# Four edits to a fused attention and mixture-of-experts kernel: wide rows for token numbers, an earlier residual load, merged masks, and one shared network moved from the tail into the last batch's body

## The reference, cut to what matters

```python
diff = a1 - lam * a2
out = einsum('bhts,bhsd->bhtd', diff, v)
out = (out - mean) * rsqrt(var + EPS)          # mean, var over all tokens of a head
h = layernorm(x + out @ Wo)                    # post-norm
router_logits = h @ router_w.T                 # top 1 of 8 experts
gate = sigmoid(topk_vals)
xs = h * gate
routed = w_down[e] @ silu_mul(xs @ w_gate_up[e])   # e: the token's expert
shared = silu_mul(h @ shared_gate_up) @ shared_down
out = layernorm(h + routed + shared)
```

## Time and profile before

| | us |
|---|---|
| median of three runs | 888.58 |
| the profiled execution, as timed | 890.63 |
| its span, first to last instruction | 888.9 |
| TensorE matmul busy | 761.6 |
| VectorE busy | 464.9 |
| ScalarE busy | 331.0 |
| GpSimd busy | 304.3 |

### The profile page before, as it was taken

The page is one execution under the profiler, slowest core; times in us unless marked ns, Lnnn a source line. Parts: engine busy times, 40 slices in busy tenths (PEclk is TensorE's granted clock), DMA queues, the critical chain, the costliest instruction groups (busy, mean ns, idle before and its releaser), DMA issues.

```text
span 888.9 us, 10662 instructions
## 1 busy us (share of the span) xinstructions
PE 761.6 (86%) x3590; PEld 381.9 (43%) x3590; DVE 464.9 (52%) x1036; ACT 331.0 (37%) x607; POOL 304.3 (34%) x262
## 2 busy tenths in 40 slices
PE   7187899997799989878998997899959867999994
PEld 3152234333244534523454353344226533666663
DVE  2765876751667765327767454774324421333332
ACT  2315443434564433255543334455613101222220
POOL 3038610123962121067510221211311204666653
PEclk9689999999799999987999899999969997999998
DMA  3753095002037220300731207000853102112100
GB/s 123 180 99 107 1 192 84 27 2 36 25 77 137 39 50 0 61 1 24 155 55 34 37 1 202 1 1 2 159 181 133 47 1 61 56 59 64 50 22 0
DMA packets 49333, 57.55 MB, mean 65 GB/s; under 512 B 11559, under 2 KB 43053, under 8 KB 47424
## 3 DMA queue, kind: packets, MB, share of 16 engines
q1 hardware_dynamic: 43024, 49.37, 25.0%
q0 software_dynamic: 3824, 6.32, 2.4%
q10 hardware_dynamic: 2432, 1.18, 0.5%
HBM read 42.67 MB, written 16.99 MB: 67 GB/s over the span
## 4 chain that ended last, share of the span: by engine, by line
PE 65%; DVE 10%; POOL 8%; DMA 7%; issue 6%; ACT 2%; SPq 0%; POOLq 0%; DVEq 0%; ACTq 0%
PE pv_ps L957 14%; PE wide_ps L1035 9%; PE s_ps L796 7%; PE wide_ps L943 7%; DVE mneg L1389 4%; PE wide_ps L783 4%; PE wide_ps L927 4%; DMA work<-x_in 3%; PE s_ps L797 3%; PE wide_ps L899 3%; PE pv_ps L1054 2%; PE misc L1054 2%; DMA slot_tokens<-tokens,slot 2%; PE misc L874 2%; PE s_ps L828 2%
## 5 line engine op out<-in xcount | busy, mean ns | idle before, releaser
L1389 DVE TENSOR_REDUCE mneg<-s_ps 128x1 f32<-128x384 f32 (+3 forms) x352 | 217.0, 638 | 105.2 <-PE s_ps L797 101.1
L1169 ACT ACTIVATE w_exp<-wide_ps 128x512 f32<-128x512 f32 x320 | 180.2, 599 | 118.9 <-PE wide_ps L943 117.6
L957 PE MATMUL pv_ps<-w_exp,work 128*64 128x512 f32 x640 | 182.3, 650 | 20.6 <-POOL w_exp L1302 18.6
L796 PE MATMUL s_ps<-w_exp 96*128 96x256 bf16 (+3 forms) x512 | 138.8, 313 | 33.5 <-DMA w_exp<-q_parts 18.3
L1302 POOL TENSOR_SCALAR_AFFINE_SELECT w_exp<-w_exp 128x1024 f32<-128x1024 f32 x64 | 70.7, 1105 | 280.7 <-ACT w_exp L1169 280.7
L943 PE MATMUL wide_ps<-w_exp 98*128 98x512 bf16 x320 | 124.0, 397 | 16.3 <-ACT w_exp L1169 15.0
L797 PE MATMUL s_ps<-mask,identb 128*128 128x128 bf16 x512 | 101.9, 227 | 0.0
L943 PEld LDWEIGHTS wide_ps<-w_exp 98*128 98x128 bf16 x320 | 31.8, 103 | 159.4 <-ACT w_exp L1169 101.3
L1035 PE MATMUL wide_ps<-w_exp,tables 128*128 x184 | 84.9, 605 | 0.0
L796 PEld LDWEIGHTS s_ps<-w_exp 96*128 96x128 bf16 x512 | 51.4, 101 | 70.9 <-DVE mneg L1389 38.8
L797 PEld LDWEIGHTS s_ps<-mask,identb 128*128 128x128 bf16 x512 | 52.3, 102 | 29.1 <-issue 5.9
(11 more groups left out here) (162 smaller groups left out, 1002.8 us busy)
## 6 DMA issues: line engine op xcount, KB each, us to landing
w_exp<-q_parts SPq DMA_DIRECT2D x96, 128.0 KB, 5.3
w_exp<-w_up_in SPq DMA_DIRECT2D x8, 1024.0 KB, 9.4
work<-x_in SPq DMA_DIRECT2D x8, 512.0 KB, 7.8
w_exp<-w_down_in SPq DMA_DIRECT2D x8, 512.0 KB, 11.5
q_parts<-w_exp SPq DMA_DIRECT2D x6, 512.0 KB, 7.0
w_exp<-k_parts SPq DMA_DIRECT2D x18, 128.0 KB, 4.0
gated_rows<-work SPq DMA_DIRECT2D x4, 512.0 KB, 3.1
x2s_rows<-x SPq DMA_DIRECT2D x4, 512.0 KB, 4.9
```

What stands on the lines that cost most here:

```text
L796: nc.tensor.matmul(o, q_stack[0:KROWS, qt, hs, :], keys[0:KROWS, gs, 0:qt + 1, :], start=True, stop=False)
L957: last = nc.tensor.matmul(pv_ps[s * 64:(s + 1) * 64, :], vo[:, kt, g, :], probs[:, n % NP, s, :], start=(kt == 0), stop=(kt == qt))
L1169: nc.scalar.activation(probs[:, n % NP, s], st_bank(v), ACT.Exp, scale=float(DH) ** -0.5).then_inc(st_done, 1)
L1389: nc.vector.tensor_reduce(out=mneg[:, qt, rows[0]:rows[-1] + 1], in_=s_ps[:, (v - 1) % 2, 0:len(rows) * w].rearrange("p (r k) -> p r k", r ...
```

## The change

Four edits.

1. **Rows of token numbers.** `slot_tokens` gets 64 equal numbers (256 bytes) for each place instead of one. VectorE spreads the numbers of a batch 64 times (`tokens_wide`, in the task `top`), and the scatter writes rows of 256 bytes. The table is filled beforehand with one number for "no token" by a DMA of 5.0 MB from SBUF on ScalarE's queue (`none_yet`), in place of a copy of 75.5 KB from DRAM. The read back takes the first number of each row.
2. **Residual load moved.** In the last body SyncE issues the residual load ahead of the loads of experts 2 and 3.
3. **Merged masks.** A bank of scores gets one mask matmul over all its rows instead of one for each.
4. **Shared network moved.** That of batch 2 goes through `SHARED` in the last body's steps 28 to 39, as in bodies 1 and 2; the `late_` tasks leave the tail. The semaphores are renamed from `late_` to `last_`.

```diff
-TAIL = [(_name, _arg, 1 if _name.startswith("late") else 0) for _name, _arg in (
-    ("norm", NUNIT - 1), ("sum", QT - 1), ("late_gate", 0), ("late_up", 0), ("mean", 0), ("late_gate", 1), ("late_up", 1), ("square", 0),
+TAIL = [(_name, _arg, 0) for _name, _arg in (
+    ("norm", NUNIT - 1), ("sum", QT - 1), ("mean", 0), ("square", 0),
...
     return [t for t in TASKS[n] if (t[2] == 0 and not (t[:2] in ONCE and post)) or (t[2] < 0 and ahead)
-            or (t[2] > 0 and post and (ahead or t[:2] not in SHARED))]
+            or (t[2] > 0 and post)]
...
-    slot_tokens = nc.dram_tensor("slot_tokens", ((E * NTOK + NROUTE) * P, 1), I32, kind="Internal").ap()
+    slot_tokens = nc.dram_tensor("slot_tokens", ((FILLS * E) * P, COPIES), I32, kind="Internal").ap()
...
-                sp.dma_start(slot_tokens, spare_d).then_inc(tokens_ready, 16)
...
                 if post:
                     store_gated(b - 1)
+                if not prep:
+                    load_residual(b)
...
-                load_residual(b)
                 if prep:
+                    load_residual(b)
                     max_rows(b + 1, 2, turned_maxima(b, 2, -1))
...
-            sp.wait_ge(late_added, QT)
+            sp.wait_ge(x2s_done, B - 1)
             store_x2s(B - 2)
...
-                sp.dma_start(rows_of[:, i:i + 1], slot_tokens[bass.ds(at * P, P), :]).then_inc(ids_loaded[g], 16)
+                sp.dma_start(rows_of[:, i:i + 1], slot_tokens[bass.ds(at * P, P), 0:1], allow_slow_non_contiguous=True).then_inc(ids_loaded[g], 16)
...
                 for n, hs in enumerate(rows):
-                    gs = hs // 4
-                    o = s_ps[:, (v - 1) % 2, n * w:(n + 1) * w]
-                    nc.tensor.matmul(o, q_stack[0:KROWS, qt, hs, :], keys[0:KROWS, gs, 0:qt + 1, :], start=True, stop=False)
-                    last = nc.tensor.matmul(o[:, w - P:w], identb[:], mask[:], start=False, stop=True)
+                    nc.tensor.matmul(o[:, n], q_stack[0:KROWS, qt, hs, :], keys[0:KROWS, hs // 4, 0:qt + 1, :], start=(n == 0), stop=False)
+                last = nc.tensor.matmul(o[:, :, w - P:w], identb[:], mask[:].unsqueeze(1).to_broadcast([P, len(rows), P]), start=False, stop=True)
...
             store_k(act, 0, 1, 3, qs, start_rest_written[1])
+            act.wait_ge(none_set, 1)
+            act.dma_start(slot_tokens.rearrange("(p n c) o -> p n (c o)", p=P, n=FILLS),
+                          none_yet.unsqueeze(1).to_broadcast([P, FILLS, E * COPIES])).then_inc(none_filled, 16)
...
-                                                 in_=tokens[:, t:t + 1], in_offset=None).then_inc(tokens_scattered, 16)
+                                                 in_=tokens_wide[:, arg], in_offset=None).then_inc(tokens_scattered, 16)
...
                 elif name == "top":
+                    dve.wait_ge(tokens_ready, 16)
+                    if b > 0:
+                        dve.wait_ge(tokens_scattered, b * QT * 16)
+                    nc.vector.tensor_copy(tokens_wide[:], tokens[:, b * QT:(b + 1) * QT].unsqueeze(2).to_broadcast([P, QT, COPIES])).then_inc(tokens_spread, 1)
```

More of the change, by code:

```diff
@@ L51 @@
 NROUTE = NTOK + E - 1
+COPIES = 64
+FILLS = 19
+assert FILLS * E >= E * NTOK + NROUTE
 WUP = DC * 2 * F
@@ L251, in build @@
 def build(nc, x, wqk, wv, wo, lams, gnw, gnb, cos_d, sin_d, ident_d, mask_d,
-          router, w_up, w_down, s_up, s_down, counts_d, tokens_d, spare_d, out):
+          router, w_up, w_down, s_up, s_down, counts_d, tokens_d, out):
     q_parts = nc.dram_tensor("q_parts", (B, 3, QT, 2, DH // 2, 16, 2, P), BF16, kind="Internal").ap()
@@ L818, in task @@
                     prep(b, arg)
-                if name in ("late_gate", "late_up", "last_gate", "last_up"):
-                    half, late = int(name.endswith("up")), int(name.startswith("last"))
+                if name in ("last_gate", "last_up"):
+                    half = int(name.endswith("up"))
                     if arg > 0:
-                        pe.wait_ge((late_silu, late_hid)[half], late * (F // P) + arg)
-                    elif late:
-                        pe.wait_ge(late_added, QT - 1 + half)
+                        pe.wait_ge((last_silu, last_hid)[half], arg)
                     for ch in range(DC):
@@ L828, in task @@
                         last = nc.tensor.matmul(s_ps[:, half], w_sh[:, at:at + P], x2T[:, ch, :], start=(ch == 0), stop=(ch == DC - 1))
[L829 to L832, removed]
+                    last.then_inc(last_full, 1)
+                if name == "last_down":
+                    hidden = shared_hidT
                     if arg == 0:
-                        pe.wait_ge(late_silu, (late + 1) * (F // P))
-                        pe.wait_ge(late_hid, (late + 1) * (F // P))
+                        pe.wait_ge(last_silu, F // P)
+                        pe.wait_ge(last_hid, F // P)
                     if arg >= 2:
-                        pe.wait_ge(late_added, late * QT + arg - 1)
+                        pe.wait_ge(last_added, arg - 1)
                     for fc in range(F // P):
@@ L840, in task @@
                                                 w_sh[:, WUP + fc * D:WUP + (fc + 1) * D], start=(fc == 0), stop=(fc == F // P - 1))
-                    last.then_inc(late_full, 1)
+                    last.then_inc(last_full, 1)
                 if name == "tail_turn":
@@ L1457, in task @@
                     dve.wait_ge(y_rstd, b * QT + arg + 1)
+                    if b == B - 1 and arg == 0:
+                        dve.wait_ge(none_filled, 16)
                     nc.vector.tensor_scalar(x2[:, b * QT + arg], y[:, arg % 2], mv[:, arg % 2, 0:1],
@@ L1462, in task @@
                     nc.vector.tensor_copy(logits[:, b * QT + arg], far[:, 0:E]).then_inc(far_done, 1)
-                elif name in ("late_up", "last_hid"):
-                    late = int(name == "last_hid")
-                    dve.wait_ge(late_full, late * (2 * (F // P) + QT) + 2 * arg + 2)
-                    dve.wait_ge(late_silu, late * (F // P) + arg + 1)
-                    hidden = shared_hidT if late else late_hidT
-                    nc.vector.tensor_tensor(hidden[:, arg], late_silus[:, arg % 2], s_ps[:, 1], ALU.mult).then_inc(late_hid, 1)
-                elif name in ("late_down", "last_down"):
-                    late = int(name == "last_down")
-                    dve.wait_ge(late_full, late * (2 * (F // P) + QT) + 2 * (F // P) + arg + 1)
+                elif name == "last_hid":
+                    dve.wait_ge(last_full, 2 * arg + 2)
+                    dve.wait_ge(last_silu, arg + 1)
+                    hidden = shared_hidT
+                    nc.vector.tensor_tensor(hidden[:, arg], last_silus[:, arg % 2], s_ps[:, 1], ALU.mult).then_inc(last_hid, 1)
+                elif name == "last_down":
+                    dve.wait_ge(last_full, 2 * (F // P) + arg + 1)
                     rows = x2[:, b * QT + arg]
-                    nc.vector.tensor_tensor(rows, rows, s_ps[:, arg % 2, 0:D], ALU.add).then_inc(late_added, 1)
+                    nc.vector.tensor_tensor(rows, rows, s_ps[:, arg % 2, 0:D], ALU.add).then_inc(last_added, 1)
                 elif name == "shared_gate":
@@ L1663 @@
           t["cos_d"], t["sin_d"], t["ident_d"], t["mask_d"],
-          t["router"], t["w_up"], t["w_down"], t["s_up"], t["s_down"], t["counts_d"], t["tokens_d"], t["spare_d"], out)
+          t["router"], t["w_up"], t["w_down"], t["s_up"], t["s_down"], t["counts_d"], t["tokens_d"], out)
     r = run(nc, [{n + "_in": v for n, v in arrays.items()}], core_ids=[0])
```

43 lines of the change are left out of this document (23 added, 20 removed).

## The result

| | before | changed kernel |
|---|---|---|
| time, median of 20 runs each, side by side | 890.6 us (885.91 to 894.0) | 886.5 us (879.62 to 890.81) |
| ratio, 95% interval | | 0.9954 (0.9933 to 0.9976) |
| profiled execution: time, span | 890.6, 888.9 us | 887.49, 885.8 us |
| mean granted clock of TensorE | 0.932 | 0.923 |

The changed kernel is 0.5% faster, which by the bound of 1% is no change. The forecast was 884.0 us, with a range of 877 to 895. The time was met, but two large effects of opposite sign lie under it, the gain of the wide rows and the cost of the moved network, and I had priced both too low.

What follows compares the result with a forecast made beforehand. TensorE was taken to bound the body, a chain of small steps and then slow scatters the tail. Terms +4.9 - 10.5 + 0.8 + 0.5 - 0.3 = -4.6 us took 888.6 to 884 us, range 877 to 895.

Steps and rivals of the forecast that it cites:

- the bound of 1%: Whole kernel: a measurement can tell about 1%, 8.9 us; chance of a time within it 0.71.
- The residual load: Last body: issued ahead of the experts, it ends GpSimd's and TensorE's wait; body's end -11.6 us, taken alone.
- The shared network in the body: Last body: twelve pieces uncovered on a full TensorE, 21.3 us plus 0.4 for the first; body ends at 666.5.
- The tail without filler: Tail: first projection at 682.7, router's maximum at 707.6 against 702.7, so +4.9 us, bounds 0 and +10.
- the half term: Tail's four token tiles: half clock would cost 10 us for all four; half of it, 5 us, was taken.
- the full-clock rival: Tail: TensorE keeps full clock, router's maximum at 702.6, time 879 us; chance 0.19.
- The rival of a tail wholly at half clock: Tail: TensorE runs wholly at half clock, time 889 us; chance 0.11.
- Rows of 256 bytes: Tail's end: scatters take 2.5 us instead of 4.4; router's maximum to second tile's first matmul 33.9 against 44.4, -10.5 us.
- the predicted hole of 2 to 3 us before the second tile: Sign at the tail's end: no 11 us hole before the first expert tile, but 2 to 3 us before the second.
- that rule: Scatters: under 512 bytes small rows stay slow at 4.4 us each, the -10.5 is gone, time 894.5 us; chance 0.13.
- Copy, fill, masks: Small terms: spreading copy in bodies 1 and 2 +0.8, fill at the start +0.5, merged masks -0.3 us.
- my bound of 1: Merged masks: 160 instructions less, -0.3 us, bounds 0 and -1.

Runs made afterwards that it cites:

- experiment 1: Kernel before with only the last body's residual load issued ahead of the experts: 875.0 us, 0.9788 of before.
- experiment 12: Changed kernel without the shared network's move and with the residual load left behind the experts: 860.99 us, 0.968 of the kernel before.
- experiment 5: Changed kernel without the move of the shared network: 860.95 us, 0.9684 of the kernel before.
- experiment 6: Changed kernel without the rows of 256 bytes: 896.87 us, 1.0085 of the kernel before.
- 3: Kernel before with only batch 2's shared network moved from the tail into the last body: 900.86 us, 1.0077 of before.
- experiment 7: Changed kernel with 21 unused matmuls added in TensorE's idle stretches of the tail: 877.49 us, 0.9863 of the kernel before.
- experiment 8: Changed kernel without the shared network's move, with rows of 32 bytes instead of 256: 861.21 us, 0.9681 of the kernel before.
- 9: Changed kernel without the shared network's move, scatter writing only the first 4 bytes of each 256-byte row: 859.27 us, 0.9679 of the kernel before.
- experiment 2: Kernel before with only the 256-byte rows for token numbers, with their fill and spreading copy: 865.05 us, 0.9676 of before.

## Why the prediction was right, point by point

- **The residual load** (-11.6 us at the body's end, taken alone): the size was right, -11.5 in experiment 1. What I gave as its cause, 3 MB of experts in front, was at most part of it. With the 4-byte scatters still there the edit did help (experiment 1), since the residual then went ahead of the stretch of low rates and landed after 5.3 us. Experiment 12 has the same 3 MB in front, the load lands after 10.5 us and costs TensorE nothing. I had divided the bytes by 394 GB/s, a rate taken from another place, and the sum did not come out: 3.5 MB at that rate are about 9 us, the load took 21.7. I should have asked where the other 12 to 13 us were; the windows of that place had the answer (89 GB/s at a DMA share of 0.82). In the changed kernel this edit should be worth nothing at all, since the rows (experiment 12 against 5) and the network in the body (6 against 3) each take away or cover the same wait; no run takes it alone out of the changed kernel.
- **The shared network in the body** (+21.3 and +0.4, body's end at 666.5): right, 665.5. All twelve pieces lie bare.
- **The tail without filler** (first projection at 682.7, maximum at 707.6): the projection was right, 682.86. The maximum came at 711.39. The term that was mis-sized is the clock: I had worked out 10 us for the four token tiles at 1.2 GHz and took half, and from 668 us on the measured tail was wholly at 1.2 GHz. From the first projection to the maximum I had 19.9 us at full clock and 24.9 with the half term; it was 28.5 in the changed kernel, and 20.0 in experiment 7. From the body's end to the maximum I had 41.1 us; it was 45.9, and experiment 7 with its clock at 1.00 had 36.8 (by the full-clock rival 702.6 - 666.5 = 36.1). What misled me was a window of before with 2.70 of 4 us busy and still at 1.00; the changed tail has windows of 2.66 to 2.91 us busy at 0.5. The one before came at a clock that was already up, those in the changed tail at one that had fallen in its first thin windows. The rival of a tail wholly at half clock was the true one in its mechanism.
- **Rows of 256 bytes** (-10.5 from the maximum to the second tile): right in kind, measured -11.8, and -13.8 in experiment 5 (44.2 against 30.4). The slowest landing was 4.2 us, and the predicted hole of 2 to 3 us before the second tile is not there: from the end of batch 3's shared network to the second tile it took 8.3 us, where I had 10.4 for the store and the gathers (0.5 of it without naming a source). The Trainium skill, page "DMA: Bandwidth & Descriptors", Specifications, has the DMA engine read, modify and write below 512 bytes; by that rule, as I read it, rows of 256, 32 and 4 bytes would all have been slow. Experiments 8 and 9 speak against it as a price for scatters: only the 4-byte writes beside each other were slow.
- **What I left out:** the rows act in the last body as well. Alone they are worth 28.6 us (experiment 2), not 10.5, and in the changed kernel that second half was invisible, since the network lay over it (S to W is 40.2 there and 40.4 without the rows, experiment 6).
- **Copy, fill, masks** (+0.8, +0.5, -0.3): the start to S was 0.2 us shorter instead of 1.0 longer. The fill landed after 19.6 us and delayed nothing that these runs can tell, and a fill of an eighth gains nothing (experiment 8). The masks may be worth 3 us, beyond my bound of 1.

So the time came out near because the rows' extra gain and the residual's both fell on a wait that the moved network covered. The tail's 4.7 us too much were mostly made up by three small misses the other way: 1.2 us before S, 0.7 from S to W and 1.3 behind the maximum. That they nearly cancel is luck, the more so as the start to S alone differs by several us between executions. As a whole the change is one edit that gives 3.2%, two that give next to nothing beside it, and one that takes 2.7% back.

## What to carry to other kernels

Work that lies in the gaps of a latency chain can be largely hidden there (three quarters of it here), and it can keep the clock up for the chain; moved into a stage that TensorE fills, all of it was paid for. When a transfer takes twice what its bytes would need at the rate seen elsewhere, look for what shares the DMA engines at that moment (a high share with few GB/s) before explaining it by the queue's order. Edits that remove the same wait don't add: try each alone and the whole without each.

## What the runs showed of the hardware

- The tail's four indirect scatters of 128 numbers landed 2.1 to 4.2 us after their issue with rows of 256 bytes (changed kernel), and after 8.5 to 17.9 us, each 4 to 5 us behind the one before it, with 4-byte rows side by side. With rows of 32 bytes, and with 4 bytes written every 256, the traces show no landing; the read back began 3.1 and 3.2 us after the last issue, as with full rows of 256 (3.2). Beside the expert loads even the rows of 256 bytes took 4.7 to 6.5 us.
- Beside 4-byte scatters the core's DMAs moved 89 to 212 GB/s, where they moved 344 to 409 beside scatters of 256-byte rows. Distances between 4 and 32 bytes were not tried, and why it is so is open.
- Twenty-one matmuls whose result nobody reads made the kernel 0.9% faster (some 8 us): the granted clock was 2.4 GHz instead of 1.2 from 668 to 700 us.
- A fill of 5.0 MB, issued at 40.84 us in the first batch's preparation and landed 19.6 us later, was not measurable: experiment 8, with an eighth of it, took the same time (0.9681 and 0.9684).
